# Loops of a graph kernel written out with constants, and selection matrices by four vector operations per unit

## The reference, cut to what matters

```python
h = jnp.maximum(_layernorm(x), 0.0)
# rounds one and two: for each edge m = ew * (h[src] @ W[edge_type]), summed over edges with the same dst
h1 = relu(segment_sum(m1, dst) + h @ root1 + b1)
x  = x + segment_sum(m2, dst) + h1 @ root2 + b2        # m2 from h1 with W2
h  = jnp.maximum(_layernorm(x), 0.0)
# round three: W3 after the sum
out = x + segment_sum(edge_weight[:, None] * h[src], dst) @ W.T + b
```

## Time and profile before

| | |
|---|---|
| median of 3 runs | 7167.74 us (7164.68 to 7173.25) |
| profiled execution, its own time | 7208.98 us |
| span of its core, first to last instruction | 7207.2 us |
| granted TensorE clock, mean | 0.576 |
| busy: POOL / PE / DVE / ACT | 4439.8 / 2694.0 / 1721.1 / 434.2 us |
| memory traffic over the span | 54 GB/s |
| round one loops, 36 units | 912.38 us, 25.34 us a unit |
| round two loops, 72 units | 1694.69 us, 23.54 us a unit |
| round three loops, 72 units | 1691.35 us, 23.49 us a unit |

### The profile page before, as it was taken

One profiled execution on the slowest core, in us unless ns is written; L12 is line 12 of the kernel. 1 busy time (PEld: TensorE's weight loads), 2 busy tenths in 40 slices (PEclk: granted clock), 3 DMA queues, 4 the chain that ended last, 5 costly groups with the idle time before them and its releaser, 6 DMA issues.

```text
span 7207.2 us, 52919 instructions
## 1 busy us (share of the span) xinstructions
PE 2694.0 (37%) x11399; PEld 2503.1 (35%) x11399; DVE 1721.1 (24%) x7377; ACT 434.2 (6%) x1186; POOL 4439.8 (62%) x4697
## 2 busy tenths in 40 slices
PE   1444444444444433333333333333333333333333
PEld 1444343443443433332333333333333333333333
DVE  4222222222222222222222222222212222112221
ACT  3100000000000000000000000000000000000000
POOL 4656566566565556666666666665666666666665
PEclk7677677776776765555555555555555555555555
DMA  4222222222222211111211111211121111112111
GB/s 124 56 55 57 56 59 58 56 57 58 55 59 55 56 50 50 50 50 49 52 50 50 50 50 50 52 50 46 49 51 51 50 50 49 50 51 51 50 50 47
DMA packets 282516, 389.08 MB, mean 54 GB/s; under 512 B 86987, under 2 KB 194904, under 8 KB 282472
## 3 DMA queue, kind: packets, MB, share of 16 engines
q0 software_dynamic: 150048, 307.60, 16.9%
q1 hardware_dynamic: 132424, 80.99, 3.8%
HBM read 336.91 MB, written 51.34 MB: 54 GB/s over the span
## 4 chain that ended last, share of the span: by engine, by line
another core or an unknown queue 45%; issue 18%; DVEq 12%; DVE 11%; DMA 7%; PE 4%; ACT 1%; SPq 0%; POOL 0%; ACTq 0%; POOLq 0%
DMA x_rows<-x 7%; DVE win L1004 5%; DVEq L1004 4%; PE bank L702 2%; DVE win L979 2%; DVE acc L916 2%; DVEq L979 1%; DVEq L908 1%; DVEq L178 1%; DVEq L916 1%; DVEq L165 1%; DVEq L930 1%; DVEq L161 1%; PE bank L637 1%
## 5 line engine op out<-in xcount | busy, mean ns | idle before, releaser
L367 POOL DMA_INDIRECT rows<-table,idx x4625 | 4376.7, 946 | 2718.7 <-issue 1407.4
L730 PE MATMUL bank<-win,rows 128*128 128x48 f32 x6252 | 1444.9, 383 | 2250.2 <-issue 2195.7
L730 PEld LDWEIGHTS bank<-win,rows 128*128 128x128 f32 x6252 | 1447.0, 323 | 2255.3 <-issue 2200.3
L916 DVE TENSOR_TENSOR acc<-acc,bank 128x48 f32 x1173 | 236.8, 202 | 4257.8 <-remote 3829.6
L702 PE MATMUL bank<-win,rows 128*128 128x192 f32 x3126 | 721.6, 384 | 556.4 <-issue 251.9
L702 PEld LDWEIGHTS bank<-win,rows 128*128 128x128 f32 x3126 | 635.6, 230 | 604.3 <-issue 334.3
L979 DVE TENSOR_SCALAR win<-iota,key,sw_col 128x192 f32<-128x192 f32 x1563 | 510.6, 388 | 79.7 <-issue 78.4
L1004 DVE TENSOR_SCALAR win<-iota,rel,sw_col 128x48 f32<-128x48 f32 x1563 | 395.7, 329 | 204.8 <-issue 204.2
L1004 DVE TENSOR_SCALAR win<-iota,rel,w_col 128x48 f32<-128x48 f32 x1563 | 387.9, 327 | 150.5 <-issue 150.5
L674 PE MATMUL bank<-ident,tile_T 128*128 128x128 f32 x98 | 45.8, 469 | 717.5 <-issue 686.7
L644 PE MATMUL bank<-ident,h_rows 128*128 128x128 f32 x98 | 36.9, 377 | 731.1 <-issue 683.4
(11 more groups left out here) (99 smaller groups left out, 1010.2 us busy)
## 6 DMA issues: line engine op xcount, KB each, us to landing
rows<-table,idx POOLq DMA_INDIRECT x4625
table<-st SPq DMA_DIRECT2D x98, 256.0 KB
table<-st SPq DMA_DIRECT2D x98, 64.0 KB
x<-st SPq DMA_DIRECT2D x98, 64.0 KB
x_rows<-x SPq DMA_DIRECT2D x98, 64.0 KB
x_rows<-in_x_dram SPq DMA_DIRECT2D x97, 64.0 KB
h_rows<-table SPq DMA_DIRECT2D x97, 64.0 KB
out_dram<-st SPq DMA_DIRECT2D x97, 64.0 KB
```

The source lines that it names most:

```text
L367: eng.indirect_dma_start(out=rows[:, slot, :], out_offset=None, in_=table[:, :], in_offset=bass.IndirectOffsetOnAxis(ap=idx[:, slot:slot + ...
L730: ins = eng.matmul(agg_ps[v][:, q * W:(q + 1) * W], rows[:, slot, :], window[:, slot, :], start=(k == 0), stop=(k == n - 1))
L916: eng.tensor_tensor(a, a, sums_ps, ALU.add).then_inc(s_acc, 1)
```

## The change

It has two parts. The loops of all engines over units and tiles become Python loops, so that the program holds every unit's instructions with constant addresses and constant semaphore values, and `hold` does nothing where its number is a constant. And `weigh` in rounds two and three makes the matrices of eight chunks at a time by two `tensor_tensor` operations over 8 x 48 columns: the first writes 1 or 0 (equal) to `match_ps` in PSUM bank 6, the second multiplies that by the weights into `window` in SBUF. Its other operand, columns 0 to 47 of `iota`, is copied to PSUM once. Each part waits for the operation before it (`s_window`, `s_eq`), and `s_window` now counts two parts a unit. The additions of groups 0 to 3 stay where they are; the two halves of `weigh` come after those of groups 1 and 2.

```diff
+        HC = UC // 2
+        iota_ps = bank[6][:, 0:W]
+        match_ps = bank[6][:, 64:64 + HC * W].rearrange("p (c w) -> p c w", w=W)
...
-        def hold(eng):
-
-            eng.sem_inc(s_hold)
+        def hold(eng, at=None):
+
+            if not isinstance(at, int):
+                eng.sem_inc(s_hold)
...
-        def units(eng, unit, whole=True):
-
-            def body(i, n):
-                for v in range(n):
-                    unit(i, v)
-            if whole:
-                body(0, RING)
-            with eng.Fori(1, NI - 2) as i:
-                body(i, RING)
-            body(NI - 2, RING)
-            body(NI - 1, last_units)
+        def units(unit, first_unit=0):
+
+            for u in range(first_unit, NU):
+                unit(u // RING, u % RING)
...
-            whole = (NT - XR) // XR
-            with eng.Fori(0, whole) as i:
-                for v in range(XR):
-                    tile1_out(i * XR + v, v, True)
-            for t in range(whole * XR, NT):
+            for t in range(NT):
                 tile1_out(t, t % XR, t < NT - XR)
...
                 def unit(i, v):
                     u = i * RING + v
-                    eng.wait_ge(s_window, u + ((r - 1) * NU + 1))
+                    eng.wait_ge(s_window, u * 2 + ((r - 1) * 2 * NU + 2))
...
-                def weigh(c, v, lo, hi, last):
-
-                    for k in range(lo, hi):
-                        ins = eng.tensor_scalar(window[:, v * UC + k, :], iota[:, 0:W], rel[:, bass.ds(c + k, 1)],
-                                                wt[:, bass.ds(c + k, 1)], ALU.is_equal, ALU.mult)
-                    if last:
-                        ins.then_inc(s_window, 1)
+                def weigh(c, v, h, n, u):
+
+                    lo, n = h * HC, min(HC, n - h * HC)
+                    slots = window[:, v * UC + lo:v * UC + lo + n, :]
+                    part = u * 2 + ((r - 1) * 2 * NU + h + 1)
+                    wait(eng, s_window, part - 1)
+                    eng.tensor_tensor(match_ps[:, 0:n, :], iota_ps.unsqueeze(1).to_broadcast([P, n, W]),
+                                      rel[:, bass.ds(c + lo, n)].unsqueeze(2).to_broadcast([P, n, W]),
+                                      ALU.is_equal).then_inc(s_eq, 1)
+                    eng.wait_ge(s_eq, part)
+                    eng.tensor_tensor(slots, match_ps[:, 0:n, :],
+                                      wt[:, bass.ds(c + lo, n)].unsqueeze(2).to_broadcast([P, n, W]),
+                                      ALU.mult).then_inc(s_window, 1)
...
                 if r == 1:
                     eng.wait_ge(s_half, 2 * NU)
+                    eng.wait_ge(s_own0_add, NT)
+                    link(eng.tensor_copy(iota_ps, iota[:, 0:W]))
                 for u in range(RING):
                     take_idx(code, u * UC, u, UC)
                 for u in range(RING):
-                    weigh(u * UC, u, 0, UC, True)
+                    for h in range(2):
+                        weigh(u * UC, u, h, UC, u)
...
-                        if ahead and q > 0:
-                            weigh(c, v, (q - 1) * n // 3, q * n // 3, q == UG - 1)
+                        if ahead and q in (1, 2):
+                            weigh(c, v, q - 1, n, u + RING)
```

More of the change, by code:

```diff
@@ L135, in build @@
         s_hold = sem("s_hold")
-        s_idx, s_window = sem("s_idx"), sem("s_window")
+        s_idx, s_eq, s_window = sem("s_idx"), sem("s_eq"), sem("s_window")
         s_row = [sem(f"s_row{k}") for k in range(NSLOT)]
@@ L328, in tile2_out @@
                 eng.dma_start(x2[bass.ds(t * P, P), :], st[:, s, D:2 * D]).then_inc(s_stored[s], 16)
-            tiles(eng, tile2_out)
+            for t in range(NT):
+                tile2_out(t, t % 2, t // 2)
             def load_x2(t, s):
@@ L344, in tile_out @@
                     load_x2(t + 2, s)
[L346 to L350, removed]
+            for t in range(NT):
+                tile_out(t, t % 2, t < NT - 2)
             for s in range(2):
@@ L374, in gather_unit @@
                 eng.wait_ge(s_idx, u + (r * NU + 1))
-                hold(eng)
                 for k in range(chunks_of(u)):
@@ L396, in fast @@
                 table_ready(r)
-                units(eng, lambda i, v: gather_unit(gathered[r], r, i, v), whole=r > 0)
+                units(lambda i, v: gather_unit(gathered[r], r, i, v), first_unit=0 if r else RING)
             def general(r):
@@ L480, in prep @@
                 wait(eng, s_fin, t + (r * NT - 1))
-                hold(eng)
+                hold(eng, t)
                 if r == 0:
@@ L533, in unit @@
                             prep(0, u - 2, v % 2)
-                units(eng, unit)
+                units(unit)
                 sums_out(NU - 1, NU - 1, 0, 2)
@@ L795, in mean_and_var @@
             def mean_and_var(e, p, sources):
-                hold(eng)
+                hold(eng, e)
                 for k, rows_k in enumerate(sources):
```

## The result

The changed kernel takes 7044.4 us in the median of 4 runs (7036.5 to 7056.3), the kernel before 7170.5 us in the same comparison (4 runs). The ratio is 0.9822, with a 95% interval of 0.9807 to 0.9837: 126 us faster, where 57 were forecast.

The account below looks back on a forecast made before the run. The prediction took POOL's gathers as the bound, with only some 1200 us of its waits to win. 42 us (registers and loops) plus 15 us (fewer instructions) made 57 off 7167.7, giving 7111 us; range 6650 to 7175.

Parts of the forecast that it names:

- The bound: On POOL: its gathers, one every 1.25 us, stay untouched, so only some 1200 us of its waits can be won.
- floor of 5968: On POOL: the time in us if all its waits went, 7168 - 1200; left out of the range.
- Registers and loops: Where POOL's wait ends: written-out code shortens the waits, by units 92 to 97 as sample; 42 us in sum.
- Fewer instructions: On DVE: twelve operations less a unit over 196 units may leave less to pile up; 15 us.
- the lower price: Gain per operation removed, from comparing rounds two and three, which have equal transfers: about 0.0066 us.
- B: Rival: the pile is made of instructions, so the upper price of 0.060 us each holds; 437 us, 6731 us; chance 0.25.
- Their direct gain: Selection matrices on DVE: four operations of 0.54 us replace sixteen, work under cover four units ahead; zero.
- The pattern of waits: POOL's waits on `idx` stay one for two units in rounds two and three, about 7.0 us, 1240 us in sum.
- At a trickle while gathers run: The other engines' instructions and semaphores get through slowly during gathers; the pile comes out about 5.4 us after POOL falls silent.
- What piles up: Either the gathers' packets or the engines' instructions; the profile doesn't say, and the gain's size hangs on it.
- C: Rival: no difference, the shorter waits were only spread or come back as a longer pile-up; 7168 us; chance 0.10.
- D: Rival: slower, fetching the written-out code holds POOL up; 93 us slower, 7261 us; chance 0.15 with other failures.

Follow-up runs that it names:

- f1: The changed kernel, unchanged, run on a second chip against the kernel before: 5919.6 us, ratio 0.9996.
- h1: The changed kernel with the old selection matrices, so only the loops are written out, on a chip with pauses: 7060.4 us, ratio 0.9837 to the kernel before.
- h2: The kernel before, loops kept, with the new four-operation selection matrices, on a chip with pauses: 7151.2 us, ratio 0.9962.
- e3: The changed kernel with POOL's semaphore increment put back before each unit's gathers, on a chip without pauses: 5922.0 us, ratio 1.0000 to the kernel before.
- f4: The changed kernel with POOL's one increment per unit put back behind its index wait, on the second chip, without pauses: ratio 1.0000 to the kernel before.
- h4: The changed kernel with POOL's one increment per unit put back before the gathers, on a fifth chip, without pauses: 5923.1 us, ratio 1.0000 to the kernel before.
- h5: The changed kernel with the old 16 small operations a unit added beside the new four, into an unread buffer, on a chip without pauses: 5923.9 us, ratio 1.0000.
- h3: The kernel before with the new selection matrices and no gathers in rounds two and three, on a chip with pauses: 3969.6 us.
- e5: The changed kernel with one or two of each group's four matmuls left out in rounds two and three, on a chip without pauses: 5921.2 us, ratio 0.9998.

## Why the prediction was right and where it was wrong

**The bound, right.** All that can be won is POOL's waits: the two chips' kinds bracket it, 7175 and 5922 us for the same kernel, with the same gathers. The forecast's floor of 5968 was 46 us too high. The forecast was drawn up for a chip with pauses, and that the comparison met such a chip again is luck: on a chip of the other kind the change is worth nothing (f1, 0.9996).

**Registers and loops, 42 us: the step that failed.** The loops alone gave 115 us. I had taken units 92 to 97 of the kernel before as a sample of written-out code, and they are, but for the increments. POOL's `hold`, one `sem_inc` between the wait and the first gather, stood in them as well. The diff takes it away everywhere; I counted `hold`s only on SP. At 0.54 us a wait and 159 waits it is 86 us, by the rows of `idx` and POOL in h1 and h2. The sample says itself that it is the increment and not the loop's branch: outside the loop the wait was shorter by the 0.3 us that I counted, and `idx` to POOL still took 0.80. With it the term would have been 42 + 86 = 128 us, against 115 measured. The two profiles' stretches of the table split the same way: of the 134 us between before and h1 (before's high profile is in them), 83 lie between `idx` and POOL, and 51 ahead of `idx`, where the 42 had counted everything. What remains argued is that each restart 0.5 us sooner is kept in the total: a run with the increment alone put back, where POOL pauses, is lacking, since e3, f4 and h4 met chips without pauses. The 51 us are not taken apart; ACT's and DVE's increments went with the loops too.

**Fewer instructions, 15 us: the right size.** The four operations alone gave 24 us (17 to 37 by the interval). That is 0.010 us for each of 2342 operations less; the lower price was 0.0066, the upper, B's, 0.060. That it is their number and not the time or the place of DVE's work is not shown; h5 was made for that and met a chip without pauses.

**Their direct gain, nothing: right under the gathers.** A new operation takes 0.56 us where 0.54 were forecast. With the gathers not pausing it is 1.000 with and without them, and with 16 operations added again; without gathers they are worth 5 us where the loops are written out, and nearly all of the 37 us of round two where they are not.

**The pattern of waits, one per two units: wrong.** It became one per three units, of 8.9 us, and the sum is 1091 us and not 1240. From this alone one would have judged that a new order of the units made the gain. h1 says no: in round two it keeps the forecast's two units and has 50 of the changed kernel's 64 us there. Why both parts together make it three is open.

**"At a trickle while gathers run": right, and now shown** by h3's two halves, with the addition that nobody could have read from the traces of one chip: it does not happen on every chip. Each chip was met in one session only, so whether it is a lasting trait of the chip or of the hour, and what makes it, no run here tells. What piles up stays open as well: e5, made for that, met a chip without pauses.

**The rivals.** B, a pile made of instructions, is refuted in its size, 437 us where 126 came: a full load of instructions without gathers runs at PE's own pace, and 2342 of them less give 24 us where its price asks for 141 (12 x 0.060 x 196). C holds on four of the chips met, by another reason than it gave: there is nothing to win. D, the fetching: nearly five times as many packets, and where POOL doesn't pause the version with nothing but the loops written out is at 1.0000 (0.9991 to 1.0009), under 6 us at most. Where it pauses, that version gained 115 us, whatever the fetching took of it. The Trainium skill (Runtime: NRT & Kernel Launch, Instruction fetch mechanics) has streams prefetched in order at little cost, and the runs agree.

## What to carry to other kernels

Count an engine's every small instruction between the semaphore that ends its wait and the work that others wait for; one increment of 0.5 us behind a wait that comes 159 times comes to 86 us by the traces, more than the 24 us of 2342 operations taken from an engine with slack. When a stretch of the old code is taken as a sample of the new, list what the change takes out and look for each item in the sample. When two changes are tested one at a time, test both orders: without the gathers either part alone took away the same gaps. And before a wait is explained, run the kernel as it is on another chip: 1250 of these 7170 us were not there on four of five.

## What the runs showed of the hardware

The kernel before takes 5921 to 5923 us on four chips, 7175 us on one, and 7170 us in the first comparison. Where it takes the longer time, single matmuls stand 2.55 us apart without a semaphore while gathers run and POOL stands idle for more than 1 us 132 to 164 times; a gather itself takes 944 to 947 ns in both. Once no gather runs, the chips are alike (4.69 matmul records each us; round three's matmuls take 707.3 us on both kinds). An increment of a semaphore on POOL costs 0.52 to 0.54 us between a wait and the first gather, on both kinds of chip; where POOL has no wait it disappears in the 305 ns between gathers. So on the chips almost without waits 294 of them cost nothing (5922.0 us against 5921.9 before).
